# Where VectorE computes a group's destination rows: in front of the output's division, or behind the next batch's score subtraction

## What is computed

```python
x = x + attention(layernorm(x), ctx)     # layer 1: rotary embedding and a window mask
x = x + experts(layernorm(x))            # top 2 of 8; layer 1 also a shared expert
```

## Time and profile before

| | |
|---|---|
| three runs | 836.37, 838.72, 839.52 us (median 838.72) |
| the profiled execution | 836.35 us; its span 834.5 us, 1.85 us around it |
| busy in the span | PE 736.1 us (88%), DVE 554.0 (66%), POOL 506.6 (61%), ACT 430.3 (52%), PEld 588.6 (71%) |
| mean granted clock of TensorE | 0.959 |
| layer 0: attention's steps 0 to 32 | about 32 to 234 us |
| layer 0: last scatters, experts | to 265 us, to about 411 us |
| layer 1: attention's steps 0 to 32 | about 427 to 636 us |
| layer 1: last scatters, experts, end | to 834.5 us |

### The profile page before, as it was taken

How to read it: one execution, slowest core, us unless ns; L and a number is a source line. 1 busy time by engine, 2 the same in 40 slices (tenths; PEclk the granted TensorE clock), 3 DMA queues, 4 the chain that set the end, 5 groups by cost and what they waited for, 6 DMA issues and landing times.

```text
span 834.5 us, 21509 instructions
## 1 busy us (share of the span) xinstructions
PE 736.1 (88%) x7184; PEld 588.6 (71%) x7184; DVE 554.0 (66%) x1682; ACT 430.3 (52%) x1040; POOL 506.6 (61%) x899
## 2 busy tenths in 40 slices
PE   3899999999982999999669999999997589999991
PEld 1677767766752999999537777777765467777770
DVE  2377888888733464444247789999985476666665
ACT  2456666565651434344235656656654546666660
POOL 7243476676754567667566447888773713777760
PEclk9999999999996999999969999999998899999996
DMA  7800000000113222222110111111210322333329
GB/s 214 359 3 2 8 21 24 25 21 22 34 33 105 59 71 73 72 73 72 58 51 23 31 39 37 57 59 38 56 46 27 89 83 64 87 89 92 90 78 296
DMA packets 65759, 58.01 MB, mean 70 GB/s; under 512 B 10611, under 2 KB 58995, under 8 KB 65110
## 3 DMA queue, kind: packets, MB, share of 16 engines
q1 hardware_dynamic: 56822, 38.27, 16.6%
q0 software_dynamic: 8704, 18.11, 6.4%
q10 hardware_dynamic: 128, 0.27, 0.1%
HBM read 34.30 MB, written 24.47 MB: 70 GB/s over the span
## 4 chain that ended last, share of the span: by engine, by line
PE 41%; POOL 25%; issue 13%; DVE 11%; DMA 3%; SPq 2%; ACT 1%; POOLq 1%; DVEq 0%
POOL results L1166 17%; PE ptp L900 12%; PE M L911 7%; PE S L886 4%; PE S L888 4%; POOL xi L1159 3%; PE M L956 3%; POOL rows L464 2%; PE M L959 2%; PE M L919 2%; DVE mx L744 1%; PE M L928 1%; SPq L1137 1%; DVE pr L745 1%; PE S L1272 1%
## 5 line engine op out<-in xcount | busy, mean ns | idle before, releaser
L539 ACT ACTIVATE pT<-ptp 77x512 f32<-77x512 f32 x256 | 138.2, 588 | 145.5 <-PE ptp L900 145.3
L1166 POOL DMA_INDIRECT results<-early,xi x144 | 151.5, 1052 | 75.9 <-DVE early L1228 70.3
L464 POOL DMA_INDIRECT rows<-out_rows,posi x128 | 126.3, 986 | 49.6 <-issue 29.0
L900 PE MATMUL ptp<-cst,pr 128*77 128x128 f32 x1024 | 138.9, 279 | 0.4
L1182 ACT ACTIVATE early<-S 128x128 f32<-128x128 f32 x176 | 48.7, 277 | 152.8 <-PE S L1265 152.8
L900 PEld LDWEIGHTS ptp<-cst,pr 128*77 128x77 f32 x1024 | 116.4, 148 | 13.7 <-ACT pT L539 8.3
L744 DVE TENSOR_REDUCE mx<-S 128x16 f32<-128x1232 f32 x64 | 91.1, 1423 | 11.0 <-PE S L888 10.9
L745 DVE TENSOR_TENSOR pr<-S,mx 128x1232 f32<-128x1232 f32 x64 | 92.2, 1441 | 2.2
L403 POOL TENSOR_TENSOR negm<-zero,mv 128x4 f32<-128x4 f32 x40 | 9.3, 232 | 128.6 <-DVE mv L627 124.0
L1272 PE MATMUL S<-W,early 128*128 (+1 forms) x208 | 81.8, 476 | 0.0
L1277 PE MATMUL S<-early,w1s 128*128 128x128 f32 x576 | 77.9, 279 | 0.6 <-ACT early L1182 0.6
(11 more groups left out here) (162 smaller groups left out, 1489.9 us busy)
## 6 DMA issues: line engine op xcount, KB each, us to landing
xs<-rows SPq DMA_DIRECT2D x144, 66.0 KB
first_w<-in_e_W SPq DMA_DIRECT2D x2, 2048.0 KB, 10.1
swap<-results SPq DMA_DIRECT2D x32, 128.0 KB, 2.2
first_w<-results SPq DMA_DIRECT2D x8, 512.0 KB, 7.3
results<-early,xi POOLq DMA_INDIRECT x144, 2.4
rows<-out_rows,posi POOLq DMA_INDIRECT x128, 2.3
rows<-out_rows SPq DMA_DIRECT2D x32, 64.0 KB, 1.6
xs<-rows SPq DMA_DIRECT2D x32, 64.0 KB
```

The lines of the kernel that those rows point to most:

```text
L464: nc.gpsimd.indirect_dma_start(rows[:, :], bass.IndirectOffsetOnAxis(posi[:, k, n:n + 1], 0), out_rows[:, ring_slot(n), k, :], None).then_ ...
L539: nc.scalar.activation(pT[:, r, :, :], ptp[r % 2][0:TK, :, :], ACT.Exp, scale=SCALE).then_inc(exp_done, 1)
L900: last = nc.tensor.transpose(ptp[r % 2][0:TK, j, :], pr[:, n % 2, r * J + j, :], ident)
L1166: nc.gpsimd.indirect_dma_start(results[:, :], bass.IndirectOffsetOnAxis(xi[:, s:s + 1], 0), ys[:, s, :], None)\
```

## The change

In a rank step below the last batch's (k under 31: six groups of layer 0, five of layer 1) `place` is no longer called at the end of `take_products(k)`, but one step later, directly behind `softmax_shift(k+1)`. The seven later groups keep their place. The semaphore values waited for are the same (`k + 3` of the rank step is `k + 2` of the step behind it).

```diff
             if k in RANK:
                 last = place_reads(RANK.index(k))
             last.then_inc(products_taken, 1)
-            if k in RANK:
+            if k in RANK and k >= B - 1:
                 place(RANK.index(k), k + 3)
...
                 before_scores(k)
             if live(k):
                 softmax_shift(k)
+                if k - 1 in RANK:
+                    place(RANK.index(k - 1), k + 2)
             if k < B:
                 router(k)
             if -2 <= k <= B + 4:
```

## The result

Five runs of the changed kernel have a median of 831.93 us (830.03 to 833.30), five of the kernel before 839.42 us (836.37 to 839.52). The ratio is 0.9924 with an interval of 0.9908 to 0.9941, so 6.4 us faster, with 4.9 to 7.7 us as bounds (the two medians differ by 7.5 us, which lies within them). The forecast was 832.5 us, faster.

A forecast was written before the change was run, and what follows sets the result against it. TensorE was taken as the bound, waiting for divided output `an` behind a held VectorE conversion. Gains of 6.4 + 0.35 + 0.3 less costs 0.6 and 0.3 gave 6.15 us: 832.5 us against the median 838.72, range 828.7 to 836.4.

The forecast's parts named there:

- The bound and the cause: Layer 0 attention: TensorE sets the pace and waits for `an` because GpSimd's instructions hold VectorE's conversion L705, 1.35 us.
- Four groups at 1.6 us: Layer 0, behind rank steps 14, 18, 22 and 26: TensorE's wait at L928 goes, 6.4 us gained in all.
- The first group: Layer 0, rank step 10, whose conversion was short: its wait of 0.35 us is gained.
- Cover for `place` in layer 0: Behind `softmax_shift`, `place` fits before L730 with 0.3 us to spare, `norms` keeps 0.4 us, conversion 0.17 us; no cost.
- Step 30's group: 0.6 us, bounds 0 and 2.7: Layer 0's sixth group: late scatters delay `norms`, L527 and, past ScalarE's pauses, L535; cost 0.6 us.
- Layer 1: gain 0.3, cost 0.3: First group's wait at L928 goes, 0.3 us gained; `place` held by GpSimd in two or three groups costs 0.3 us.
- Sum: Whole kernel: 7.05 us removed less costs of 0.6 and 0.3 gives 6.15 us faster.
- Rival A: `place` held in its new place too, group six's scatters cost their bound; only 2.35 us gained, 836.4 us; chance 0.14.
- Rival C: `an` comes early but something else holds TensorE for the same 1.6 us; time stays at 838.7 us; chance 0.04.
- Rival B: GpSimd becomes the bound through late scatters in layer 0's six moved groups; 9.1 us slower, 847.8 us; chance 0.06.

The follow-up runs named there:

- no_conversion_old_place: Kernel before, nothing moved, the sum L704 writing row numbers as unsigned integers so conversion L705 falls away in all 18 groups; 830.62 us, ratio 0.991.
- the three runs above: `conversion_only`, `no_conversion_new_place` and the change: L527 2.37, 2.57 and 2.78 us later than before, L535 not late, 0.18 and 0.38 us late.
- layer_1_only: Kernel before with `place` moved only for the five groups of layer 1; 838.13 us, ratio 0.9988.
- no_conversion_new_place: Changed kernel with the sum writing the row numbers itself and no conversion; 829.8 us, ratio 0.9899.
- conversion_only: Kernel before with only the conversion L705 moved behind the next score subtraction in the same eleven groups, rest of `place` unmoved; 834.3 us, ratio 0.9942.
- four_groups: Kernel before with `place` moved only for rank steps 14, 18, 22 and 26 of layer 0; 832.67 us, ratio 0.9921.
- keep_step_30: Changed kernel, but layer 0's group of rank step 30 keeps its old place; 831.42 us, ratio 0.9909 against the kernel before.
- end_of_next_step: Changed kernel with `place` of the eleven groups later still, at the end of `take_products(k+1)`; 842.24 us, ratio 1.0057 against the kernel before.

## Why the prediction was right, point by point

- **The bound and the cause.** VectorE's conversion was held by GpSimd, and TensorE waited for the division behind it. `no_conversion_old_place` shows it by itself: without the conversion the wait falls from 1.56 to 0.19 us, with everything in its old place.
- **Four groups at 1.6 us.** Measured 1.61 us in the two steps behind rank step 14. The first group gave 0.39 us (its two steps 6.56 + 5.80 became 6.06 + 5.91), forecast 0.35. Together 6.86 us in the loop against 6.75. What I didn't see is that the price has two parts, 1.26 us for the conversion and 0.2 to 0.3 for the place.
- **Cover for `place` in layer 0.** 0.3 us to spare before L730 was forecast, 0.27 measured; 0.4 before `norms`, 0.45 measured; the conversion at 0.17 us in all six groups.
- **Step 30's group: 0.6 us, bounds 0 and 2.7.** Measured 1.08 in the profiled pair. `norms` came 3.15 us late (forecast 3.1) and L527 2.78 (2.7), both counted from the row operation of step 33, and L535 0.38 us late, where I had left 0.6. The term that was mis-sized is ScalarE's slack: I added up its pauses to 2.07 us, and the three runs above show 2.4. The other 0.7 us of the 1.08 are a fall of the granted clock (0.5 us) and one long scatter (0.2), which I hadn't counted. They aren't shown to be the change's: `layer_1_only` has both without it, and `no_conversion_new_place` and `conversion_only`, which move the group's conversion too, don't have the fall. That 0.6 lies between the 0.4 that are shown and the 1.1 of the pair of traces is partly luck.
- **Layer 1: gain 0.3, cost 0.3.** The loop is 0.49 us longer in after. 0.59 us of that lie in the step from 10 to 11, in front of the first moved group: 6.19 us in before, 6.78 in after, and 6.77 in `four_groups`, in which layer 1 is untouched. So they aren't the change's. The two steps behind rank step 12 went from 12.64 us (`four_groups`: 12.65) to 12.28 in after, and to 12.27 in `keep_step_30` and `layer_1_only`: a gain of 0.36, forecast 0.3. What is left over, 0.25 us in after and 0.1 in the other two, is the cost, forecast 0.3. VectorE was held where it was expected, for up to 0.55 us in L702 and 0.73 in L705 beside GpSimd's work, and TensorE hardly felt it. Timeline of after, step 17 of layer 1:

```profile
529.96 0.55 DVE L702 TENSOR_TENSOR posk<-oh,pos 128x64 f32<-128x64 f32 x1
...
530.78 0.72 POOL L416 TENSOR_TENSOR kexp<-kT,cst 128x308 f32<-128x308 f32 x1
530.79 0.73 DVE L705 CAST posi<-posf 128x8 uint32<-128x8 f32 x1
```

- **Sum.** 6.15 us was forecast. The pair of traces gives 6.86 - 1.08 + 0.36 - 0.25 = 5.9 us, and 6.6 without the 0.7 that may be chance; the ratio gives 6.4 (4.9 to 7.7).
- **Rival A** needed a conversion that is held in the new place too. It is short in all six groups of layer 0, and the group of step 30 cost 1.1 us, not 2.7. **Rival C** falls with the waits. **Rival B** did not happen in the change. I had named 4.3 us of delay of the scatters as the point from which GpSimd decides in layer 0. Counted from the row operation behind rank step 14 the first scatter starts at +0.85 in before (123.71 - 122.86), at +3.61 in after (a delay of 2.76, forecast 2.7) and at +5.86 in `end_of_next_step` (127.67 - 121.81, a delay of 5.0). This last kernel is slower than before, but in layer 0's loop TensorE didn't wait for GpSimd even there; so the threshold isn't confirmed. The rival's mechanism shows in layer 1 alone, where I hadn't placed it: TensorE waits for `qT`, and the loop is 6.7 us longer.

What stays open is, first, why the conversion wasn't let go at the end of the scatter. In before it was held to 122.17, past the scatter's end at 121.23 and to the end of L414 at 122.12. No run separates a lock that is kept over several instructions from one that GpSimd wins again at each of them. Second, not every conversion beside GpSimd's work is held. Behind rank step 10 of before it started beside L414 and took its usual time:

```profile
96.37 0.32 POOL L414 TENSOR_TENSOR bias_qk<-negA,swap 128x77 bf16<-128x77 f32 x1 [1.28 <-issue]
...
96.59 0.17 DVE L705 CAST posi<-posf 128x8 uint32<-128x8 f32 x1
```

Another of before, at 251.24 us and half the size, started 0.48 us into a scatter and took 0.17 us as well. What decides it, no run shows. The Trainium skill, "SBUF — State Buffer", section "Who interferes with whom", lists casts as an operation that can take the shared ports, and says that on trn2 a `tensor_reduce` never contends; the sums of 0.22 us beside scatters in `no_conversion_old_place` agree. Its rule that the loser waits for the whole instruction of the other gives 0.4 us where the row has 1.35, and there the measurement decides.

## What to carry to other kernels

When a tiny instruction's longest time is many times its median, look at what ran on the neighbouring engine while it was open; if that is the cause, changing the instruction's kind (here a sum that writes whole numbers, instead of a sum and a conversion) is worth as much as moving it, and it leaves the order alone. When a producer is moved later, count the idle time of the engine that waits for it up to its next duty, in every stage; and count again what the moved work now stands in front of on its own engine. A delay of 2.8 us fitted here. One of 5.0 us turned a gain of 6 us into a loss of 5, in layer 0 through VectorE's own lateness, in layer 1 through GpSimd's. For a pair of traces, split the difference by landmarks before explaining it, since a stage in which the clock rises by chance can move 2 to 3 us.

## What the runs showed that I had not expected

- At the end of layer 0 the granted clock fell to 0.50 for some three microseconds in after, behind a wait of 0.96 us, and a pair of products took 0.79 instead of 0.49 us. It fell there in `end_of_next_step` (a wait of 1.65 us) and also in `layer_1_only`, whose wait was the usual 0.58 us, and not in `no_conversion_new_place`, which waited 0.76. The longer wait isn't shown to be the reason.
- At the start of layer 1 the clock came back later in some executions than in others, whatever the kernel, which moved the same stretch between 177.7 and 180.8 us.
- Beside the same scatter, a product of two buffers and a sum took 0.24 and 0.22 us, a conversion of eight numbers a partition, started later in it, 1.35 us. In layer 1 a product was held too, beside GpSimd's tensor operations (0.55 us for L702).
